# Cross-attention and mixture-of-experts kernel in fp32: the next batch's first score group is moved into the wait for the shift rows

## The reference, cut to what matters

```python
def _attn(q, k, v):
    s = jnp.einsum('bhqd,bhkd->bhqk', q, k) * SCALE
    p = jax.nn.softmax(s, axis=-1)
    return jnp.einsum('bhqk,bhkd->bhqd', p, v)
...
q = _ln((x @ Wq + bq).reshape(b, s1, H, HD), qn_w, qn_b)
...
k = _ln(kv[..., :HD], kn_w, kn_b)
...
ctx = ctx + DCA_WEIGHT * ctx_dca
return ctx @ Wo + bo
...
x = x + _L0_xattn_ref(_layernorm(x, axis=-1), ctx_1024, ...)
x = x + _L0_ffn_ref(_layernorm(x, axis=-1), ...)
```

## Time and profile before

| | |
|---|---|
| runs | 1031.34 us median of 3 (1030.19 to 1031.38) |
| profiled execution | 1032.6 us, span in the profile 1030.8 us |
| busy share of the span | PE 90%, DVE 74%, ACT 57%, POOL 41% |
| granted TensorE clock | 0.967 of full speed, mean |
| DMA | 116.55 MB, mean 113 GB/s, q1 (SP and ACT) 40.4% of 16 engines' span |

### The profile page before, as it was taken

One profiled execution on the slowest core, in us unless ns is written; L12 is line 12 of the kernel. 1 busy time (PEld: TensorE's weight loads), 2 busy tenths in 40 slices (PEclk: granted clock), 3 DMA queues, 4 the chain that ended last, 5 costly groups with the idle time before them and its releaser, 6 DMA issues.

```text
span 1030.8 us, 17520 instructions
## 1 busy us (share of the span) xinstructions
PE 923.9 (90%) x5148; PEld 658.7 (64%) x5148; DVE 758.9 (74%) x1717; ACT 588.5 (57%) x1621; POOL 425.6 (41%) x288
## 2 busy tenths in 40 slices
PE   4687999999999999999999999558799999999998
PEld 2354655655655655655655655325699899998997
DVE  6756777777777777877778777375678878788784
ACT  2237877868778678678668779547223223232231
POOL 4953753754744735736636637471000000000000
PEclk9888999999999999999999999767899999999999
DMA  9356345455365365274374364833311111111111
GB/s 277 80 141 142 99 135 127 124 145 123 110 161 123 95 176 118 86 178 114 96 174 111 93 148 103 271 128 129 121 63 45 57 61 61 61 41 61 61 41 41
DMA packets 51581, 116.55 MB, mean 113 GB/s; under 512 B 8984, under 2 KB 17560, under 8 KB 51288
## 3 DMA queue, kind: packets, MB, share of 16 engines
q1 hardware_dynamic: 50280, 115.28, 40.4%
q10 hardware_dynamic: 816, 0.79, 0.3%
q0 software_dynamic: 448, 0.03, 0.3%
HBM read 47.24 MB, written 17.30 MB: 63 GB/s over the span
## 4 chain that ended last, share of the span: by engine, by line
PE 58%; DVE 15%; ACT 11%; DMA 8%; issue 4%; POOL 3%; DVEq 0%; ACTq 0%; SPq 0%
PE f_ring L1659 13%; PE f_ring L1603 11%; ACT sc L1000 8%; PE sc L847 7%; DVE pm L1179 7%; PE ring L759 7%; DMA QS<-s_lo 6%; PE ring L862 5%; PE ring L879 3%; PE sc L808 3%; PE ring L774 3%; POOL vs L582 2%; ACT xT L977 1%; PE ring L785 1%; PE f_ring L1630 1%
## 5 line engine op out<-in xcount | busy, mean ns | idle before, releaser
L582 POOL TENSOR_TENSOR vs<-vs,neg_half 128x16 f32<-128x16 f32 x66 | 198.7, 3034 | 199.5 <-DVE vs L1142 199.4
L1000 ACT ACTIVATE sc<-sc,nm 128x240 f32<-128x240 f32 x512 | 225.7, 455 | 33.0 <-DVE ed L1184 32.9
L1179 DVE TENSOR_REDUCE pm<-sc 128x64 f32<-128x1024 f32 x128 | 156.3, 1221 | 50.7 <-PE sc L808 47.5
L1009 ACT ACTIVATE pt<-sc 128x1024 f32<-128x1024 f32 x128 | 124.2, 1024 | 39.7 <-PE sc L847 39.7
L1715 ACT ACTIVATE hb<-hb 128x352 f32<-128x352 f32 x64 | 31.9, 498 | 186.6 <-DVE hb L1765 186.6
L808 PE MATMUL sc<-KS,QS 96*128 96x256 f32 x512 | 99.8, 318 | 33.7 <-ACT sc L1000 33.7
L808 PEld LDWEIGHTS sc<-KS,QS 96*128 96x128 f32 x512 | 72.2, 194 | 88.6 <-ACT sc L1000 73.7
L759 PE MATMUL ring<-wq,xT 128*128 128x512 f32 x256 | 119.8, 611 | 8.8 <-ACT xT L977 4.2
L879 PE MATMUL ring<-wo,ot 128*128 128x512 f32 x256 | 122.1, 601 | 0.7 <-DVE ot L1240 0.7
L1000 ACT ACTIVATION_READ_ACCUMULATOR sc<-sc,nm 128x1 f32 x512 | 116.5, 228 | 0.0
L847 PE MATMUL sc<-QS,KS 100*128 100x256 f32 x512 | 82.6, 305 | 10.6 <-DMA QS<-s_lo 10.3
(11 more groups left out here) (175 smaller groups left out, 1864.5 us busy)
## 6 DMA issues: line engine op xcount, KB each, us to landing
QS<-q_hi SPq DMA_DIRECT2D x128, 128.0 KB, 2.3
KS<-k_hi SPq DMA_DIRECT2D x128, 128.0 KB, 2.3
xin<-in_x_dram SPq DMA_DIRECT2D x16, 512.0 KB, 3.5
QS<-q_lo SPq DMA_DIRECT2D x64, 128.0 KB, 2.3
KS<-k_lo SPq DMA_DIRECT2D x64, 128.0 KB, 2.3
xres<-in_x_dram SPq DMA_DIRECT2D x16, 512.0 KB, 3.3
x_scratch<-xres SPq DMA_DIRECT2D x16, 512.0 KB, 3.8
x<-x_scratch SPq DMA_DIRECT2D x16, 512.0 KB, 3.2
```

Of the source, the lines that this page charges most:

```text
L582: pool.tensor_tensor(w, w, neg_half[0:rows, :], ALU.pow).then_inc(rstd, 1)
L1000: last = act.activation(s, s, ACT.Exp, bias=nm[:, t, h:h + 1], accum_out=den[:, t, h:h + 1])
L1009: act.activation(pt[g % 2][:, (p % 2) * 2:(p % 2) * 2 + 2, :], sc[p % 2][:, :, :], ACT.Exp).then_inc(sc_evac[p % 2], 1)
L1179: dve.tensor_reduce(pieces, s.rearrange("p h (c n) -> p h c n", n=DCA), AX_X, ALU.max, negate=True).then_inc(g_max, 1)
```

## The change

It moves the following.

- **Score groups.** Group 0 of batch b + 1 is issued on PE right after LT of batch b, its maxima on DVE right after `s_lo`, its exponentials on ACT right after the `s_lo` DMA. Group 1 takes its old place before `values` 3. A stage so begins with group 2. `group_at` and `pair_at` give the new counts: group 1 waits till pair 7 has been read out.
- **k earlier.** `k_transposes` comes right after group 2, ahead of the value projections, ACT's `kf` right after exponentials 1; `V0` and `V1` are copied out later. Ring banks (`HOME`) change accordingly, `x_transposes` comes before group 7, the output projection's halves one group later, `k_high` and `residual` 0 one group later.
- **k's low part.** Its four stack DMAs go to POOL's queue, with a semaphore of their own (`k_lo_in`); a tiny add into `mark` carries the wait.
- **Output bias.** The add on `xres` moves on POOL from the end of stage b to stage b + 1, between `dca_keys` and `k_low`.
- **The end.** The last expert's split in stage last comes after the gate's row roots and waits for `lt_rdy`. SP loads the feed-forward's rows of batch 0 at the end of stage later and those of batch 1 (buffer `x2_1`, now allocated before) in stage last. The biases `b2_b` are loaded without waiting for the rows' stores.

```diff
+    def group_at(b, k):
+        if k % G == 0 and k < G:
+            return 8 * b - 4 if not isinstance(b, int) or b > 0 else 0
+        return 8 * b + k // 2
+
+    def pair_at(step, b, p):
+        return 8 * b + 4 + p // 2 + (1 if p % 2 == 0 and step in AHEAD else 0)
```

On SP:

```diff
             if step in ATTN:
                 sp.wait_ge(sh_hi, b + 1)
                 shift_rows(sp, par, s_hi, 0)
+            if step == "last":
+                moe.load_rows(sp, 1)
...
             if step == "later":
+                sp.wait_ge(q_in, STACKED * B)
+                sp.wait_ge(k_in, K_STACKED * B)
+                sp.wait_ge(k_lo_in, K_LO_STACKED * B)
+                moe.load_rows(sp, 0)
```

On POOL:

```diff
         def k_low(m):
             pool.wait_ge(k_hi_rdy, m + 1)
+            wait(pool, k_lo_in, K_LO_STACKED * m)
...
+            if step in WOUT:
+                output_bias(b - 1)
+            if step in KEYED:
                 k_low(b + 1)
+                pool.wait_ge(k_lo_rdy, b + 2)
+                pool.tensor_tensor(mark[:, :], eps_ln[:, :], eps_ln[:, :], ALU.add)
+                stack_rows(pool, KS[1 - par], k_lo, 2, k_lo_in)
...
             if step == "last":
                 moe_constants()
                 for e in range(moe.NE):
+                    if e == moe.NE - 1:
+                        moe_row_root()
+                        pool.wait_ge(lt_rdy, B)
                     split_first(e)
-                    if e == moe.NE - 3:
-                        moe_row_root()
```

On PE:

```diff
             if attn:
-                scores(b, par, 1)
+                scores(b, par, 2)
+            if keyed:
+                k_transposes(step, b)
...
             if attn:
                 shift_transposes(step, b)
+            if step in AHEAD and attn:
+                scores(b + 1, 1 - par, 0)
...
             if step in AHEAD and attn:
-                scores(b + 1, 1 - par, 0)
+                scores(b + 1, 1 - par, 1)
```

On ACT:

```diff
             if attn:
                 wait_evac(act, step, "LT", b)
                 shift_rows(act, par, s_lo, 2)
+            if step in AHEAD and attn:
+                exps(b + 1, 0)
...
+            if step == "p2":
+                exps(0, 0)
             if proj:
                 wait(act, q_lo_rdy, b + 2)
```

On DVE:

```diff
-            group_max(b, 1)
+            group_max(b, 2)
             if keyed:
                 q_high(b + 1)
...
             dve.tensor_tensor(s_lo[:, :], bank[0:2 * H, 0:S], s_hi[:, :].bitcast(F32),
                               ALU.subtract).then_inc(taken(step, "LT"), 1)
+            if step in AHEAD:
+                group_max(b + 1, 0)
```

More of the change, by code:

```diff
@@ L99, in bass_xattn_moe @@
         with ExitStack() as stack:
-            attention_phase(nc, stack, shared, early, even, odd, moe, x, ctx, Wq, bq, Wk, bk, Wv, bv, Wdca,
+            maxima = maxima_buffers(nc, stack, x, ctx)
+        moe.add_second_rows(nc, outer)
+        with ExitStack() as stack:
+            attention_phase(nc, stack, shared, early, even, odd, maxima, moe, x, ctx, Wq, bq, Wk, bk, Wv, bv, Wdca,
                             bdca, qn_w, qn_b, kn_w, kn_b, kd_w, kd_b, Wo, bo, x2_dram, vd_dram)
@@ L155, in stacked_buffers, with maxima_buffers @@
     return buffers
+def maxima_buffers(nc, stack, x, ctx):
+    T, G, TOK = x.shape[1] // P, H // HP, ctx.shape[1]
+    buffers = {}
+    for name, shape in (("pm", [P, T, HP, G, TOK // DCA]), ("ed", [P, T, HP, G, DCA])):
+        buffers[name] = stack.enter_context(nc.sbuf_tensor(name, shape, F32))
+    return buffers
 class MoeInputs:
@@ L439, in squares_of_head, with stack_rows @@
         return vs[0:values.shape[0], k, 0:values.shape[1]]
+    def stack_rows(eng, stacks, part, blk, done):
+        for h in range(HP):
+            eng.dma_start(stacks[blk * HD:(blk + 1) * HD, h, :, :].bitcast(F32),
+                          part[h * HD:(h + 1) * HD, :, :].bitcast(F32)).then_inc(done, 16)
     def shift_rows(eng, par, part, row):
@@ L482, in load_vdca @@
                          vd_dram[bass.ds(m, 1)].rearrange("b k n -> (b k) n")).then_inc(v_ld[par], 16)
-        def stack_rows(tensor, par, part, blk, done):
-            for h in range(HP):
-                sp.dma_start(tensor[par][blk * HD:(blk + 1) * HD, h, :, :].bitcast(F32),
-                             part[h * HD:(h + 1) * HD, :, :].bitcast(F32)).then_inc(done, 16)
         def load_x(m):
@@ L513, in body @@
                 sp.wait_ge(q_hi_rdy, b + 2)
-                stack_rows(QS, 1 - par, q_hi, 0, q_in)
-                stack_rows(QS, 1 - par, q_hi, 2, q_in)
+                stack_rows(sp, QS[1 - par], q_hi, 0, q_in)
+                stack_rows(sp, QS[1 - par], q_hi, 2, q_in)
                 sp.wait_ge(q_lo_rdy, b + 2)
-                stack_rows(QS, 1 - par, q_lo, 1, q_in)
+                stack_rows(sp, QS[1 - par], q_lo, 1, q_in)
                 sp.wait_ge(k_hi_rdy, b + 2)
-                stack_rows(KS, 1 - par, k_hi, 0, k_in)
-                stack_rows(KS, 1 - par, k_hi, 1, k_in)
-                sp.wait_ge(k_lo_rdy, b + 2)
-                stack_rows(KS, 1 - par, k_lo, 2, k_in)
+                stack_rows(sp, KS[1 - par], k_hi, 0, k_in)
+                stack_rows(sp, KS[1 - par], k_hi, 1, k_in)
                 if step == "p2":
@@ L607, in normalise_k, with output_bias @@
                                    ALU.mult).then_inc(k_norm, 1)
+        def output_bias(m):
+            pool.wait_ge(r_ld, 16 * (m + 1))
+            pool.wait_ge(wo_ld, 32)
+            pool.tensor_tensor(xres[:, :, :], xres[:, :, :],
+                               bo_b[:, :].unsqueeze(1).broadcast_to([P, T, D]),
+                               ALU.add).then_inc(res_rdy, 1)
         def row_root(m):
@@ L1042, in body @@
             if attn:
+                exps(b, 2)
+            if keyed and attn:
+                copy_out(step, b, "V0", v[1 - par][0:ROWS[0], 0:1, :], D)
+            if attn:
                 exps(b, 3)
                 dca_exps(b, 0)
+            if keyed and attn:
+                copy_out(step, b, "V1", v[1 - par][0:ROWS[1], 1:2, :], D)
+            if attn:
                 exps(b, 4)
                 exps(b, 5)
+                exps(b, 6)
             if proj:
@@ L1234, in k_high @@
             dve.wait_ge(kd_rdy, b + 2)
-            wait(dve, k_in, STACKED * (b + 1))
+            wait(dve, k_in, K_STACKED * (b + 1))
             dve.tensor_copy(k_hi[:, :, :], kf[:, :, :]).then_inc(k_hi_rdy, 1)
@@ L1416, in body @@
                 return
-            group_max(b, 1)
+            group_max(b, 2)
             if keyed:
                 q_high(b + 1)
-            for k in (2, 3, 4):
-                group_max(b, k)
+            group_max(b, 3)
+            if step == "last":
+                moe_row_stats()
+            group_max(b, 4)
+            group_max(b, 5)
             if keyed:
                 k_high(step, b)
-            group_max(b, 5)
-            if step == "last":
-                moe_row_stats()
+            group_max(b, 6)
             if wout:
                 residual(step, b, 0)
-            group_max(b, 6)
             group_max(b, 7)
```

117 lines of the change are left out of this document (54 added, 63 removed).

## The result

The changed kernel takes 1047.88 us, median of 4 runs (1044.34 to 1048.0), against 1031.36 us for the kernel before (1030.19 to 1031.73): a ratio of 1.0154, 95% interval 1.0131 to 1.0177. It is slower by 16.5 us; the forecast of 1033.1 us and its range, 1023 to 1044, both miss.

What follows compares the result with a forecast made beforehand. The prediction took a chain of waits through PE, DVE and ACT, 39.43 us a period, as the bound. Its terms, 4.0 + 0 + 3.8 - 0.9 - 5.1 + 2.9 - 2.9 = +1.8, gave 1033.1 us, range 1023 to 1044.

Steps and rivals of the forecast that it cites:

- Steady periods: The 13 attention periods between shift transposes: their terms sum to +0.31 us each, +4.0 in all.
- The first group of part (c): Score-group round after pairs and values: its first group, now group 1, waits for pair 7's buffer, +0.56 us a period.
- PE in the wait: Wait for the `s_lo` DMA: group 0 takes 0.68 us on PE with 0.28 free before the first pair, +0.4 a period.
- Gain taken: 0: Group 0's 1.77 us of exponentials move into ACT's idle, but a later group comes forward instead, so nothing is gained.
- the tail: End of a steady period: x's transposes and one output half change places about group 7, +0.05 us.
- R1: Slower rival: k's low part lands late and group 0 holds PE's line in each period; +19.5, 1053 us; chance 0.18.
- The start: First batch: group 0's exponentials have no earlier batch to hide in and run ahead of q's affine copies, +3.8 us.
- Stages later and last: A group less gives -0.9 in stage later; stage last gains -1.6, and its delayed split -0.6 and -2.9; -5.1 together.
- `f_xh`: Last batch: the delayed POOL split meets this DVE instruction and holds it as it held `wln`, +2.9 us.
- R2: Faster rival: the round of groups gets shorter by one in every steady period; -15.6, 1017.5 us; chance 0.12.
- R3: Mildly faster rival: `f_xh` slips ahead (-2.9) and half of the start's term is hidden (-1.9); 1028.3 us; chance 0.15.
- main case: The likeliest outcome, with the summed terms about as forecast: 1029.3 to 1037 us, chance 0.55.

Runs made afterwards that it cites:

- The banks' experiment: The changed kernel with one edit, v's first half of outputs in ring bank 1 and its second in bank 2, instead of 2 and 1: 1036.04 us.
- the three kernels with the old order and the side parts: Changed kernel with engine order, banks and counts as before: 1014.94 us; that with the bias add back: 1027.18; that with k_lo's DMAs on SP's queue: 1014.91.

## Why the prediction was wrong

By the steps of its own sum:

- **Steady periods, +0.31 forecast: +1.22 measured.** Here it failed. The larger part is a step that was not there: the wait for k's transposes and `kf` was priced nowhere in the steady part, and there was no term for TensorE's clock. The prediction took the order of `kf` ahead of v as free, though the new `HOME` gives V0 the bank that KT1 has just filled, so that PE has to wait for the ACT copy. The wait is 0.55 us, worth 0.1 a period by itself; the fall of the clock behind it, in 10 of 13 periods, is worth about 0.9 each. The banks' experiment shows both. Of the 13.5 us by which the forecast's sum falls short of the span, the falls are 8.7 (10 x 0.87), the wait itself 1.4 (13 x 0.11), the start 2.1. The rest of the order was priced nearly right: without the clock and the bank it costs 39.88 - 38.63 = 1.25 us a period, where the forecast's terms for it add up to 0.4 + 0.56 + 0.05 = 1.01.
- **"The first group of part (c)", +0.56, and "PE in the wait", +0.4.** Together 0.96. Group 1 starts at 445.13 - 428.57 = 16.56 us after LT where group 0 started 271.44 - 256.11 = 15.33 after, 1.2 later. The size of the sum was nearly right; the first pair came 5.77 - 5.55 = 0.2 later and not 0.4, and the wait that the forecast named, for `pt` of pair 7, is there with 0.55 us.
- **"Gain taken: 0" for the exponentials.** Right, but for half of the reason. The six groups ahead of x's copies were one bound; PE, with a half of the output projection moved to the place behind group 7, was another that stood ahead of it; the term "the tail", +0.05, held this move and did not see a bound in it. Either alone removed brings 0 to 0.2 us a period, both together 1.55. A chain of waits shows one of two such bounds.
- **The bias add, -0.7.** Right: -0.84 by the experiment with the add back (in the old order), against bounds of 0 and -0.95.
- **k's low part, 0.** Right: landing in 3.8 us, between the 2.3 and the 5.0 of the earlier trace rows, and group 0 with no wait. R1, 18 in 100, did not happen, though the time came out on its side. The estimate that the Trainium skill ("DMA: Bandwidth & Descriptors", Specifications) allowed, 2.7 us, was 1.1 too low for these transfers of 128 KB.
- **The start, +3.8: +5.9 measured.** The mechanism, one more group ahead of x's copies, is shown by x's copies a group earlier (5.1 us sooner). That exponentials ahead of `qf` matter is refuted, and with k's transposes as before the first LT came only 0.5 sooner. The size was too small: the forecast had ACT through group 4 at 89.5, and it got there at 90.9. Of these 1.4 us, 1.25 are a wait of ACT for v's matmuls, which take 0.63 us here; from 75 to 85 us the granted clock is 0.50, where it was 0.95 before. The forecast priced them, and Q0 (5.30 us for its eight matmuls, 4.55 before; the row below has the first five), at the durations of before. That the clock makes this part is argued from the rows; no run took it away. Against the three kernels with the old order and the side parts (first LT at 96.4 to 97.9) the start even costs 5.8 to 7.3.

```profile
86.09 0.60 ACT L1021 ACTIVATE v<-ring 128x512 f32<-128x512 f32 x1 [1.25 <-PE ring L817]
```

```profile
83.72 0.63 PE L817 MATMUL ring<-wkv,cT 128*128 128x512 f32 x1
...
96.48 4.01 PE L802 MATMUL ring<-wq,xT 128*128 128x512 f32 x5 [2.45 <-ACT xT L1021]
```

- **Stages later and last, -0.9 and -5.1: -0.5 and -4.6.** Right, with some luck in the second: the split does let `wln` through (0.19 to 0.23 us in all twelve kernels that have it so), but the stage took 38.5 to 43.6 us in the eight other kernels with group 0 in the wait, so that one execution does not fix this term to better than 1 us.
- **`f_xh`, +2.9: 0 here.** This, too, was luck, and to the good. Of the twelve profiled executions with the delayed split (the changed kernel and the eleven of the experiments), nine had `f_xh` at 0.98 us and three at 3.94 or 3.95. "All or nothing" was right and the choice wrong; it should have been a chance. The Trainium skill ("SBUF — State Buffer", Who interferes with whom) calls it an exclusive lock whose holder is set by the order of issue: the starts, 0.06 us behind POOL's in the three and 0.15 us ahead of it here, agree.
- **Feed-forward, -2.9.** The rows are there, and the first output matmul comes 754.23 - 740.70 = 13.53 us after the phase's first matmul instead of 740.33 - 723.76 = 16.57: -3.0. But from there to the end it lost 1.4 again, so that the phase gained 1.6. PE now waits for DVE's splits of W2 and shows matmuls at 0.63 us behind that wait:

```profile
754.23 0.49 PE L1711 MATMUL f_ring<-w_hi,hT_hi 128*128 x1 [1.88 <-DVE w_lo L1789]
...
755.34 0.63 PE L1711 MATMUL f_ring<-w_lo,hT_hi 128*128 x1
```

That this wait holds back the 1.4 us is argued from these rows; no run took it away.

R2 was rightly put low: no steady period of the changed kernel got shorter by a group. Of R3, `f_xh` did slip ahead, but its half of the start did not come. The sign, with slower at 0.43, was on the right side by luck: 0.18 of that was R1, whose landing was never waited for, and 0.25 was the upper part of the main case, while what made the kernel slower stood in no case. The range was closed at 1044 by k's landing alone, with no case for the clock.

## What to carry to other kernels

When an order is changed, go through the ring's banks as through the engines: for each matmul ask who last filled its bank and what empties it, since a copy that stood safely far ahead can come to stand right before it. Where a group is moved out of a round and nothing gets shorter, look for a second bound behind the first, and move both before giving the idea up. Measure the parts of a bundled change apart: here one POOL instruction, moved from ahead of `q_lo` to behind it, was worth 12 us, and the order hid it by costing 33.

## What the runs showed of the hardware

- The granted clock fell from 1.00 to a mean of 0.57 over 4 us behind two waits of 0.87 and 0.55 us on PE, in 10 of 13 periods of one execution, and in 11 of 13 of another. Of the three periods without a fall in the first, two had the same 0.87 and 0.55 us to 0.01; the third had only 0.25 us in place of the 0.87. What makes the difference is open. With k's order as before, four periods had a wait of 1.49 to 1.52 us, and one of the four a fall behind it; waits of 0.88 and 0.89 us with 2 us of work between them, in the kernel of the banks, were followed by none. So neither one wait nor its length decides alone; that the second wait close behind the first matters is shown by its removal.
- POOL's queue landed 128 KB 3.8 us after issue, SP's in 2.3 to 2.4, in one and the same execution (medians). It is no fixed gap: `k_hi` on SP's queue took 3.0 us in the kernel of the banks and 3.5 in that with k's order as before, where POOL's `k_lo` took 3.7 and 3.6.
- A DVE cast of 128x1024 begun 0.7 to 1.6 us before the end of a POOL add took 1.26 to 2.13 us instead of 0.68, and ended 0.54 to 0.56 us behind the add in all 26 steady periods of two kernels. Not every POOL instruction does this: beside `vs<-vs,neg_half`, in the kernel before at 45.2 and 77.1 us, the same cast took 0.66 and 0.68 us. A `tensor_scalar` that began 0.06 us behind POOL's subtraction took 3.94 instead of 0.98; begun 0.15 us ahead, it took 0.98 and POOL's 3.86 instead of 3.15.
